# Local scores of a transformer stack on 64 by 32 tiles of the array, with two score blocks of a tile joined into one

## The reference

```
qkv = shift_tokens(x) @ Wqkv[i]             # 128 -> 3 x 1024, 16 heads of 64
q = l2norm(q) * qs;  k = l2norm(k) * ksc    # per head
q, k = rotated by position, with a scale (and its inverse) per position
sim  = q @ k2^T * 8                          # windows of 32: each window sees itself and the one before
attn = softmax(where(mask, -big, sim))
x = concat_heads(attn @ v2) @ Wo[i] + x
x = (a * gelu(gate)) @ W2[i] + b2[i] + x     # a, gate from layernorm(shift_tokens(x)) @ W1[i] + b1[i]
```

## Time and profile before

| | |
|---|---|
| median of three runs | 3594.57 us (3592.30 to 3594.88) |
| span of the profiled execution, its own time | 3598.4 us |
| PE busy | 3482.8 us (97%), 33868 matmul records |
| weight loads (PEld) busy | 2390.4 us (66%) |
| DVE busy | 3160.0 us (88%) |
| ACT busy | 3061.0 us (85%) |
| POOL busy | 2352.0 us (65%) |
| chain that ended last | PE 62%, ACT 19%, issue 10%, DVE 5% |
| granted PE clock, mean | 0.998 |

### The profile page before, as it was taken

How to read it: one execution, slowest core, us unless ns; L and a number is a source line. 1 busy time by engine, 2 the same in 40 slices (tenths; PEclk the granted TensorE clock), 3 DMA queues, 4 the chain that set the end, 5 groups by cost and what they waited for, 6 DMA issues and landing times.

```text
span 3598.4 us, 95666 instructions
## 1 busy us (share of the span) xinstructions
PE 3482.8 (97%) x33868; PEld 2390.4 (66%) x33868; DVE 3160.0 (88%) x5848; ACT 3061.0 (85%) x5121; POOL 2352.0 (65%) x1607
## 2 busy tenths in 40 slices
PE   8999899999999999999999999999999999999998
PEld 6777466666666666666666666666666666666666
DVE  6998889888988988888888898888889888888986
ACT  5766688888888888888888888888888888888886
POOL 2001677777777777777777677777777777777774
PEclk9999999999999999999999999999999999999999
DMA  2000011112211112211112111112111112211112
GB/s 63 0 0 0 21 34 39 38 33 54 52 34 34 39 36 52 50 40 33 34 40 53 46 39 38 32 36 58 47 33 39 38 33 55 52 33 34 39 37 54
DMA packets 182965, 136.67 MB, mean 38 GB/s; under 512 B 97612, under 2 KB 135632, under 8 KB 182800
## 3 DMA queue, kind: packets, MB, share of 16 engines
q1 hardware_dynamic: 180019, 125.00, 14.8%
q10 hardware_dynamic: 2781, 9.51, 0.9%
HBM read 19.04 MB, written 2.10 MB: 6 GB/s over the span
## 4 chain that ended last, share of the span: by engine, by line
PE 62%; ACT 19%; issue 10%; DVE 5%; SPq 1%; POOL 1%; DMA 1%; ACTq 0%; DVEq 0%; POOLq 0%
PE ps L1302 12%; PE ps L1389 10%; PE ps L1356 10%; PE ps L1344 7%; PE ps L1379 4%; PE ps L1370 4%; PE ps L1160 3%; ACT L750 3%; ACT area L603 2%; DVE area L987 2%; ACT G L609 2%; ACT L609 2%; ACT area L618 2%; ACT area L625 2%; PE ps L1295 2%
## 5 line engine op out<-in xcount | busy, mean ns | idle before, releaser
L1302 PE MATMUL ps<-Wqkv,xsT 128*128 128x512 f32 x2304 | 1112.5, 605 | 8.7 <-ACT area L638 3.8
L449 POOL TENSOR_TENSOR area<-area,tab 128x512 f32<-128x512 f32 x768 | 970.0, 1273 | 146.7 <-ACT area L618 146.1
L1302 PEld LDWEIGHTS ps<-Wqkv,xsT 128*128 128x128 f32 x2304 | 391.2, 189 | 351.4 <-issue 295.0
L462 POOL TENSOR_TENSOR area<-area,lsum 128x1024 f32<-128x1024 f32 x192 | 365.5, 1904 | 383.2 <-DVE lsum L916 383.2
L456 POOL TENSOR_TENSOR AQb<-AQb,area 128x1024 f32<-128x1024 f32 x192 | 455.2, 2371 | 15.1
L456 POOL TENSOR_TENSOR area<-area 128x1024 f32<-128x1024 f32 x192 | 455.0, 2370 | 9.0 <-DVE area L976 1.5
L618 ACT ACTIVATE area<-ps 128x1024 f32<-128x1024 f32 x384 | 393.6, 1025 | 66.2 <-PE ps L1302 55.1
L1389 PEld LDWEIGHTS ps<-kbd,area 128*32 128x32 f32 x12288 | 313.2, 109 | 196.1 <-issue 113.4
L1344 PE MATMUL ps<-BD,area 128*64 128x128 f32 x6144 | 421.5, 279 | 17.7 <-issue 11.3
L1344 PEld LDWEIGHTS ps<-BD,area 128*64 128x64 f32 x6144 | 329.4, 137 | 158.8 <-issue 100.2
L1389 PE MATMUL ps<-kbd,area 128*32 128x128 f32 x12288 | 415.6, 276 | 17.0 <-ACT kbd L648 5.7
(11 more groups left out here) (136 smaller groups left out, 6630.6 us busy)
## 6 DMA issues: line engine op xcount, KB each, us to landing
BD<-area SPq DMA_DIRECT2D x1344, 64.0 KB, 2.0
Vx<-area SPq DMA_DIRECT2D x384, 32.0 KB, 1.9
Wqkv<-ffn_Wqkv ACTq DMA_DIRECT2D x18, 512.0 KB, 4.0
BB<-area SPq DMA_DIRECT2D x384, 16.0 KB, 1.8
x2s<-x2s SPq DMA_DIRECT2D x96, 56.0 KB, 2.0
Wo<-ffn_Wo SPq DMA_DIRECT2D x6, 512.0 KB, 4.3
W<-ffn_W SPq DMA_DIRECT2D x6, 341.0 KB
x2s<-x2s SPq DMA_DIRECT2D x96, 0.2 KB, 1.7
```

The source lines that it names most:

```text
L449: pool.tensor_tensor(b4[:, :, here], q4[:, :, there], s4[:, :, here], ALU.mult).then_inc((s_bq, s_bk)[j], 1)
L462: pool.tensor_tensor(p3, p3, lsum[:, 1, :].unsqueeze(2).broadcast_to([P, HEADS, 2 * WIN]), ALU.mult).then_inc(s_pn, 1)
L1302: last = mm(PJ[:, b * 512:(b + 1) * 512], xsT[:, par, t * P:(t + 1) * P], Wqkv[:, w0:w0 + 512], start=True, stop=True)
```

## The change

Turned keys are kept plainly in kT, the 64 channels of the even head over those of the odd one, without zeros. `k_evac` becomes one instruction over 128 partitions. The scores of a tile t are one call of 64 matmuls, each of 64 rows (one head), 32 columns and 64 moving columns; even heads go to bank 0 and odd heads to bank 1, so `row_max` and `less_max` of index g handle the even or the odd heads and `less_max` writes them to alternate places of Pr. The semaphore s_sc counts one per tile in place of two. The call for tile 0 stands behind `output(n-2,1)`, where the second of its two calls was, and that for tile 1 behind `project_k(n,0)`, likewise. The orders of ACT, DVE, POOL and SP stay.

```diff
-        kbd = sb("kbd", [P, PAIRS, 2, WIN + SEQ])
+        kT = sb("kT", [P, PAIRS, WIN + SEQ])
...
-                        pool.memset(kbd[:, :, :, :], 0.0).then_inc(i_zero, 1)
+                        pool.memset(kT[:, :, :], 0.0).then_inc(i_zero, 1)
...
                 need(act, s_tr[g], turn_of_k(n, t))
-                need(act, s_sc, 4 * n - 1 + g)
-                c = slice(4 * g, 4 * g + 4)
+                need(act, s_sc, 2 * n)
                 at = slice(WIN + P * t, WIN + P * t + P)
-                act.activation(kbd[0:DH, c, 0, at], tr[0:DH], ACT.Copy)
-                act.activation(kbd[DH:P, c, 1, at], tr[DH:P], ACT.Copy).then_inc(s_te[g], 1)
+                act.activation(kT[:, 4 * g:4 * g + 4, at], tr, ACT.Copy).then_inc(s_te[g], 1)
...
                 need(act, s_tr[g], turn_of_q(n, t))
-                need(act, s_sc, 2 * T - 1 + g)
+                need(act, s_sc, T)
...
-            s3 = SC.rearrange("p a (h k) -> p a h k", k=2 * WIN)
+            s3 = SC.rearrange("p a (c k) -> p a c k", k=2 * WIN)
...
-                need(dve, s_sc, 2 * T + g + 1)
+                need(dve, s_sc, T + 1)
...
-                dve.tensor_tensor(Pr[:, t, 512 * g:512 * g + 512].rearrange("p (h k) -> p h k", k=2 * WIN), s3[:, g, :, :],
+                dve.tensor_tensor(Pr[:, t, :].rearrange("p (c a k) -> p c a k", a=2, k=2 * WIN)[:, :, g, :], s3[:, g, :, :],
...
-            def scores(n, t, g):
-
-                need(pe, s_mk, 4 * n + 2 * t + g + 1)
-                need(pe, s_te[g], turn_of_k(n, 1) if t else turn_of_q(n, 0))
-                for c in range(4 * g, 4 * g + 4):
-                    for w in range(NWIN):
-                        k0 = P * t + WIN * w
-                        last = mm(SC[32 * w:32 * w + 32, g, (c % 4) * P:(c % 4 + 1) * P],
-                                  qT[:, c, 32 * w:32 * w + 32], kbd[:, c, :, k0:k0 + 2 * WIN],
-                                  start=False, stop=True, skip_group_check=True)
+            def scores(n, t):
+
+                need(pe, s_mk, 4 * n + 2 * t + 2)
+                for g in range(2):
+                    need_apart(pe, i_pe, s_te[g], turn_of_k(n, 1) if t else turn_of_q(n, 0))
+                    for c in range(4 * g, 4 * g + 4):
+                        for w in range(NWIN):
+                            k0 = P * t + WIN * w
+                            for a in range(2):
+                                half = slice(DH * a, DH * a + DH)
+                                last = mm(SC[32 * w:32 * w + 32, a, c * 2 * WIN:(c + 1) * 2 * WIN],
+                                          qT[half, c, 32 * w:32 * w + 32], kT[half, c, k0:k0 + 2 * WIN],
+                                          start=False, stop=True, skip_group_check=True)
                 last.then_inc(s_sc, 1)
...
-                if mid:
-                    scores(n - 1, 0, 0)
                 if ffn:
                     output(n - 2, 1)
                 if mid:
-                    scores(n - 1, 0, 1)
+                    scores(n - 1, 0)
                     turn_q(n - 1, 1, 0)
                     turn_q(n - 1, 1, 1)
                     turn_k(n - 1, 1, 0)
...
                 if mid:
-                    scores(n - 1, 1, 0)
                     turn_k(n - 1, 1, 1)
...
                 if mid:
-                    scores(n - 1, 1, 1)
+                    scores(n - 1, 1)
```

More of the change, by code:

```diff
@@ L139, in build @@
         nmx = sb("nmx", [P, 2, HA])
-        names = ("d_x d_x2 d_wa d_wap d_rot d_c d_wq d_wk d_wv d_qks d_wo d_ln d_ff d_out i_const i_zero i_pad i_dve i_pool i_sp i_guess i_bits d_id d_wav d_hm "
+        names = ("d_x d_x2 d_wa d_wap d_rot d_c d_wq d_wk d_wv d_qks d_wo d_ln d_ff d_out i_const i_zero i_pad i_dve i_pool i_sp i_pe i_guess i_bits d_id d_wav d_hm "
                  "a_lnc a_lnr a_lnn a_xh a_xt a_xe a_qk a_qe a_ke a_km a_v a_ve a_s a_mx a_e a_t a_te "
@@ L149, in build @@
         S = {n: sem(n) for n in names.split()}
-        (d_x, d_x2, d_wa, d_wap, d_rot, d_c, d_wq, d_wk, d_wv, d_qks, d_wo, d_ln, d_ff, d_out, i_const, i_zero, i_pad, i_dve, i_pool, i_sp, i_guess, i_bits, d_id, d_wav, d_hm,
+        (d_x, d_x2, d_wa, d_wap, d_rot, d_c, d_wq, d_wk, d_wv, d_qks, d_wo, d_ln, d_ff, d_out, i_const, i_zero, i_pad, i_dve, i_pool, i_sp, i_pe, i_guess, i_bits, d_id, d_wav, d_hm,
          a_lnc, a_lnr, a_lnn, a_xh, a_xt, a_xe, a_qk, a_qe, a_ke, a_km, a_v, a_ve, a_s, a_mx, a_e, a_t, a_te,
```

## The result

The kernel after takes 4215.88 us (median of four, 4215.34 to 4217.59), against 3594.73 us for the kernel before in the same session (3592.30 to 3597.73). The ratio is 1.1729, 95% interval 1.1712 to 1.1745: 621 us or 17% slower. The forecast was 4075 us with a range of 3930 to 4330 us.

A forecast was written before the change was run, and what follows sets the result against it. TensorE, 97% busy, was taken as full only because its block order covers waits; 3.9 us of waits net of saved work plus 1.2 us of clock over 94 steps gave 4078 us profiled, 4075 us median, range 3930 to 4330 us.

The forecast's parts named there:

- The order: TensorE's new gaps before output, turn of k, projection of k and turn of xn: 0.78, 1.7, 0.95, 3.1 us.
- the walk: One step's waits traced: 6.5 us of gaps, less 1.98 work, 0.35 old gap, 0.3 old waits: +3.9 us a step.
- The clock: Half clock behind the 3.1 us gap before the turn of xn in every step: 1.2 us a step, 113 us.
- The rival of a second fall: The 1.7 us gap before the turn of k also lowers the clock: 4197 us, chance 0.12.
- the rival of none: No fall of the clock behind the gaps: 3961 us, chance 0.15.
- The block: A joined score block of 1.03 us replaces two of 1.01 us, saving 1.98 us of TensorE work a step.
- row halves overlap: Both row halves of a score block work at once; the rival, taking turns, gave 4245 us, chance 0.10.
- The rival of feeding: Score-block records are fed no faster than the old average, 4.04 us a block: 4640 us, chance 0.05.

The follow-up runs named there:

- e2: Kernel before, old tiles and block-diagonal keys, with the two score calls of a tile joined in the changed kernel's order: 4266.35 us, ratio 1.1862.
- e1: Changed kernel with DVE's first max of tile 1 moved behind the layer norm: 3944.37 us, ratio 1.0968.
- e8: e2 with twelve extra bf16 matmuls of 512 columns filling the gap before the turned xn: 4175.10 us, ratio 1.1604.
- e3: Changed kernel with twelve extra bf16 matmuls of 512 columns filling the gap before the turned xn: 4160.01 us, ratio 1.1571.
- e4: Changed kernel with each score matmul over only the 32 keys of its own window, half the columns: 4222.36 us in one run.
- e6: e2 with 64 small float32 matmuls of 16 columns in the gap before the turned xn, lengthening the program: 4305.36 us, ratio 1.1966.
- e12: Changed kernel with the hardware loops of two steps written out on every engine: 4135.73 us, ratio 1.1509.

## Why the prediction was right, and where it was off

**The order.** Right, step by step: gaps of 0.70, 1.64, 0.76 and 2.93 us against 0.78, 1.7, 0.95 and 3.1, each with its releaser. In sum they are 6.0 us against the 6.5 of the walk. e2 shows that the order costs this with the old tiles as well, e1 that the largest part hangs on DVE's max of tile 1.

**The clock.** Right in kind: half clock behind the 2.93 us gap, none behind the 1.64 us gap, 122 us by e8's price against 113 us. The rival of a second fall is out by the first of the three stretches, the rival of none by the third. That the sizes agree so well is in part luck. The prediction had a fall in every step, and 37 of the 96 gaps brought none. And e1 and e3, in which this gap is gone or filled, still have a mean clock of 0.988, some 100 us of half clock, where e8 with its short program has 0.998. So the gap accounts for about 225 of the 306 us, 90 us of time, and the other 80 us, some 30 us of time, stand at places that the prediction did not count: 13 of the 78 stretches at 0.50 follow a wait before the turned x behind a jump. The Trainium skill (TensorE: Matmul & The Clock Gate, Part 4) has transposes not count as busy in the same way; eight of them precede the gap of 1.64 us here, and the stretch behind it was at 1.00.

**The block.** Mis-sized: "With 0.056 us a burst that is 0.89 us, and with 0.14 us for the ends a block of 1.03 us". It took 1.44 us, so the work saved is 2 x (2 x 1.01 - 1.44) = 1.16 us a step, not 1.98: 77 us over the 94 steps. That row halves overlap was right (one at a time would be 1.93 us or more). What failed is the step to sustained feeding: "four matmuls of one burst start within 0.03 us" is the pace of the records that stand ready. It held for the first 30 records and no longer, and e4 shows that the columns are not what slows the rest. The rival of feeding had the right cause with a far too high price. The Trainium skill (TensorE: Matmul & The Clock Gate, Part 1) has starts no closer than about 25 ns; here two records of a float32 matmul began every 21 ns, and in the first 0.23 us one record every 7.7 ns, so between tiles that distance does not hold.

**What was not counted.** The program's length. The prediction saw "The number of records per step rises by 128 pairs" and asked only how fast they are fed. The body of the loop no longer stays loaded. While one layer's loop turns (1218.5 to 1539.6 us, four passes) the kernel after moves 36 packets of instructions, and over a loop of the kernel before (1082.5 to 1347.2 us) it moves none. e6 puts the price at some 70 us and e12 at some 75 us with the loops' own cost. The Trainium skill (Runtime: NRT & Kernel Launch, Instruction fetch mechanics) says that a jump to code that is not in the loaded pages has to wait for its fetch. The trace agrees for the kernel after, with 30 gaps of 0.6 to 2.5 us behind 30 jumps; the kernel before makes the same 30 jumps with no gap there.

**The sum, from the ledger of TensorE.** Waits for ACT and DVE at the four places rose by 535 us (574 - 39). The score blocks fell by 94 x 2 x (2.02 - 1.44) = 109 us. Half clock adds 122 us. TensorE's other idle time, before the values, the scores, the turned k of tile 0, the turned x and the turned q, rose from 51 us (17.7, 17.0, 16.1, 0 and 0) to 110 us (12.1, 18.7, 24.5, 46.3 and 7.9), and 90 us of it are now put down to issue: 59 us. 535 - 109 + 122 + 59 = 607 us; the spans differ by 4213.9 - 3598.4 = 615.5 us. The page allows a check of the halves: 535 + 59 = 594 us is the whole rise of the idle time, and busy time rose by 3504.3 - 3482.8 = 21.5 us where the blocks and the clock give 122 - 109 = 13 us, so what is left lies in busy time. Against the forecast the blocks are 77 us more, the other idle time 59 us and the clock 9 us, the waits some 15 us less (535 against 94 x (6.5 - 0.35 - 0.3) = 550): 130 of the 141 us by which it was short. The waits came out as forecast at each of their places, so no errors cancel there; the clock's total did so in part by luck, as said above.

## What to carry to other kernels

When two blocks that cover different waits are joined, look first at what read the earlier one alone: everything behind that reader in its engine's order is late by the distance between the blocks, and this can cost several times what the joining saves. Smaller tiles mean more instructions, and they have two prices beside the array's: the pace at which matmuls are fed once those standing ready are used up, and whether a loop's body still stays loaded. Here these prices ate up what the shorter blocks saved, and only the single copy of each key was a gain. Before moving a wait, walk the whole period to the next covered wait of every engine, for that is where the time turns up again.

## What the runs showed of the hardware

- Small float32 matmuls on different tiles begin 7.7 ns a record at first (30 records in 0.23 us), and then one record every 10.8 ns with a pause of 0.1 us in it. Matmuls of 16 columns on four column tiles came one record every 8.3 ns (e6).
- A loop body that has grown from about 320 to 450 records a step (two steps a pass) is fetched anew in each pass: 410 packets of 16 KB against 98, 9 packets a pass in one layer's loop where the kernel before moves none, with 0.6 to 2.5 us of waiting before the turned x behind each jump back. Written out, the same program has no wait there and moves 345 packets.
- One microsecond at half clock cost 0.4 us of time in this kernel: 93 us for some 235 us of it (e8 against e2), 32 us for 83 us among the runs of e12.
